# The last attention's gates as 24 more columns of its query, key and value product

## The reference

```python
h = x * rsqrt(mean(x * x, -1) + 1e-06) * norm_w
q, k, v = heads(Wq), heads(Wk), heads(Wv)          # h @ W.T, 128 columns each, 8 heads of 16
q, k = _apply_rope(q, cos, sin), _apply_rope(k, cos, sin)
beta, ig, og = gate(Wbeta, bbeta), gate(Wig, big), gate(Wog, bog)   # sigmoid(h @ W.T + b), 8 columns each
# over the tokens of a sequence:
M = M * f_t + g_t * scale * (k_t[:, None] * v_t[None, :])
y_t = (q_t @ M) * o_t
y = y @ Wout.T + bout
```

## Time and profile before

| what | before |
|---|---|
| median of 3 runs | 1366.78 us (1364.93 to 1370.55) |
| profiled execution | 1362.23 us, span of its instructions 1360.4 us |
| busy, share of the span | TensorE 88%, VectorE 78%, ScalarE 59%, GpSimd 50% |
| mean granted TensorE clock | 0.957 |

### The profile page before, as it was taken

How to read it: one execution, slowest core, us unless ns; L and a number is a source line. 1 busy time by engine, 2 the same in 40 slices (tenths; PEclk the granted TensorE clock), 3 DMA queues, 4 the chain that set the end, 5 groups by cost and what they waited for, 6 DMA issues and landing times.

```text
span 1360.4 us, 39548 instructions
## 1 busy us (share of the span) xinstructions
PE 1202.4 (88%) x14377; PEld 906.5 (67%) x14377; DVE 1059.4 (78%) x3479; ACT 808.9 (59%) x1351; POOL 678.0 (50%) x727
## 2 busy tenths in 40 slices
PE   2857888899889888888987899999989999999997
PEld 1524766676767666666766677877777777677765
DVE  4888789988787988798878787775786688876662
ACT  1545667546745655545655686675866566656562
POOL 0167657777677776778777653314243255210010
PEclk9987998999999998999998999999989899899897
DMA  9002433432344232223434321221200010000001
GB/s 317 1 32 65 112 99 86 121 93 89 97 124 124 64 100 69 83 75 86 105 93 116 89 62 37 57 56 46 55 25 26 10 41 25 25 11 9 11 2 32
DMA packets 172958, 94.13 MB, mean 69 GB/s; under 512 B 98539, under 2 KB 163206, under 8 KB 172646
## 3 DMA queue, kind: packets, MB, share of 16 engines
q1 hardware_dynamic: 112838, 34.26, 10.4%
q0 software_dynamic: 16384, 33.59, 8.8%
q10 hardware_dynamic: 43552, 23.74, 5.9%
HBM read 25.98 MB, written 45.61 MB: 53 GB/s over the span
## 4 chain that ended last, share of the span: by engine, by line
PE 46%; DVE 28%; ACT 9%; issue 6%; POOL 5%; SPq 3%; DMA 2%; ACTq 0%; POOLq 0%; DVEq 0%
PE bank L701 12%; PE bank L746 4%; PE bank L760 3%; POOL rows L1714 3%; SPq L1780 2%; DVE heads_store L975 2%; DVE x L1007 2%; PE sums L934 2%; PE bank L717 2%; PE bank L556 2%; PE bank L917 2%; PE bank L729 1%; DVE stats_head L964 1%; PE bank L748 1%; PE bank L786 1%
## 5 line engine op out<-in xcount | busy, mean ns | idle before, releaser
L1731 POOL DMA_INDIRECT y_in<-ys,r_result x256 | 276.8, 1081 | 131.4 <-issue 71.2
L1714 POOL DMA_INDIRECT rows<-store,r_slot x256 | 261.9, 1023 | 84.7 <-issue 76.1
L701 PE MATMUL bank<-u_xp,w_hi 128*128 128x128 f16 x2432 | 271.1, 225 | 15.3 <-DMA u_xp<-rows 4.4
L701 PE MATMUL bank<-u_xp,w_lo 128*128 128x128 f16 x1216 | 247.3, 222 | 0.0
L701 PEld LDWEIGHTS bank<-u_xp,w_hi 128*128 x2432 | 166.4, 99 | 64.0 <-issue 24.4
L701 PEld LDWEIGHTS bank<-u_xp,w_lo 128*128 x1216 | 119.8, 99 | 3.0
L1683 POOL TENSOR_SCALAR ve_front<-mv_front 128x4 f32<-128x4 f32 x16 | 3.1, 194 | 180.6 <-DVE mv_front L968 180.4
L556 PE MATMUL bank<-heads_store,w_hi 128*128 128x512 f16 x256 | 81.1, 400 | 7.2 <-DVE x L1043 3.1
L1484 ACT COPY heads_store<-bank 128x512 f32<-128x512 f32 x64 | 37.2, 586 | 73.8 <-PE bank L506 52.8
L746 PE MATMUL bank<-heads_store,f_w1s 128*128 128x512 f32 x128 | 74.7, 667 | 0.9 <-ACT heads_store L1591 0.9
L1007 DVE SCALAR_TENSOR_TENSOR x<-y_in,r_weight,x 128x128 f32<-128x128 f32 x256 | 72.6, 345 | 1.7 <-DMA y_in<-ys,r_result 0.5
(11 more groups left out here) (389 smaller groups left out, 3257.4 us busy)
## 6 DMA issues: line engine op xcount, KB each, us to landing
ys<-u_y_even ACTq DMA_DIRECT2D x38, 256.0 KB
ys<-u_y_odd ACTq DMA_DIRECT2D x38, 256.0 KB
u_xp<-rows SPq DMA_TRANSPOSE x304
x<-x_dram SPq DMA_DIRECT2D x16, 256.0 KB, 5.6
rows<-store,r_slot POOLq DMA_INDIRECT x256
y_in<-ys,r_result POOLq DMA_INDIRECT x256
out_dram<-x SPq DMA_DIRECT2D x16, 256.0 KB, 2.3
rows<-blank SPq DMA_DIRECT2D x48, 64.0 KB
```

Of the source, the lines that this page charges most:

```text
L701: ins = pe.matmul(B[:, of_block[j]], of_expert(wp, e, 2 * part + which), xp_rows[:, xp, of_block[j]], start=(n == 0 and j == 0), stop=(n = ...
L1714: pool.indirect_dma_start(row_dram[g], bass.IndirectOffsetOnAxis(route.slot[g][:, i, t:t + 1].bitcast(U32), 0), rows[:, groups[g].first * ...
L1731: pool.indirect_dma_start(fetch.y[i][:, t, k, :], None, y_dram[g], bass.IndirectOffsetOnAxis(route.result[g][:, k, t0 + t:t0 + t + 1].bitc ...
```

## The change

The two weights become one tile of 408 columns, and TensorE makes for each of the four tiles of tokens one product of 408 columns in place of one of 24 and one of 384; the gates are columns 384 to 407 of each of the four banks. VectorE reads them there with four instructions that multiply by `rstd` and add the bias at once, in place of one multiplication and one addition over all four tiles. ScalarE's copies of a bank also ask for VectorE's instruction on that bank, but a later one of it has been waited for by then. The written order of the steps (`turns`) stays.

```diff
-        a1_wqkv = sb("a1_wqkv", [P, 3 * D])
-        a1_wg = sb("a1_wg", [P, 3 * NH1])
-        a1_mean = sb("a1_mean", [P, 3 * D + 3 * NH1])
+        a1_w = sb("a1_w", [P, 3 * D + 3 * NH1])
+        a1_wqkv, a1_wg = a1_w[:, 0:3 * D], a1_w[:, 3 * D:]
...
-                    pe.matmul(M[:, 64:64 + 3 * D], minus_mean[:], a1_wqkv[:], start=True, stop=True)
-                    prep.by_tensor.mark(pe.matmul(M[:, 64 + 3 * D:64 + 3 * D + 3 * NH1], minus_mean[:], a1_wg[:],
-                                                  start=True, stop=True), "a1")
+                    prep.by_tensor.mark(pe.matmul(M[:, 64:64 + 3 * D + 3 * NH1], minus_mean[:], a1_w[:], start=True,
+                                                  stop=True), "a1")
...
                 elif k == 1:
-                    G = 3 * NH1
                     on.wait_ge(*s.by_scalar.at("xt", "attn1", c))
-                    B = bank(s.name, "z", c)
                     on.wait_ge(*prep.by_vector.at("a1_centred"))
                     for t in range(T):
-                        ins = pe.matmul(B[:, t * G:(t + 1) * G], s.xt[:, by_t[t]], a1_wg[:], start=True,
-                                        stop=True)
-                    s.by_tensor.mark(ins, "z", c)
-                    ring.free_at((s.name, "z", c), s.by_vector, "z", c)
-                    for t in range(T):
                         B = bank(s.name, "qkv", c, t)
-                        s.by_tensor.mark(pe.matmul(B[:, 0:3 * D], s.xt[:, by_t[t]], a1_wqkv[:], start=True,
+                        s.by_tensor.mark(pe.matmul(B[:, 0:3 * D + 3 * NH1], s.xt[:, by_t[t]], a1_w[:], start=True,
                                                    stop=True), "qkv", c, t)
                         ring.free_at((s.name, "qkv", c, t), s.by_scalar, "v", c, t)
...
-                    dve.tensor_tensor(a1_wg[:], a1_wg[:], mean[:, 3 * D:], ALU.add)
-                    mark(dve.tensor_tensor(a1_wqkv[:], a1_wqkv[:], mean[:, 0:3 * D], ALU.add), "a1_centred")
+                    mark(dve.tensor_tensor(a1_w[:], a1_w[:], mean, ALU.add), "a1_centred")
...
                 elif k == 1:
-                    on.wait_ge(*s.by_tensor.at("z", c))
                     on.wait_ge(*s.by_pool.at("rstd", "attn1", c))
-                    mark(dve.tensor_tensor(s.z, ring[s.name, "z", c][:, 0:T * G].rearrange(
-                        "p (t g) -> p t g", t=T), wide(s.rstd[:], G), ALU.mult), "z", c)
-                    on.wait_ge(*at("z", c))
-                    mark(dve.tensor_tensor(s.z, s.z, const["a1_bg"][:].unsqueeze(1).broadcast_to([P, T, G]),
-                                           ALU.add), "zb", c)
-                    on.wait_ge(*at("zb", c))
+                    for t in range(T):
+                        on.wait_ge(*s.by_tensor.at("qkv", c, t))
+                        mark(dve.scalar_tensor_tensor(s.z[:, t, :], ring[s.name, "qkv", c, t][:, 3 * D:3 * D + G],
+                                                      s.rstd[:, t:t + 1], const["a1_bg"][:], ALU.mult, ALU.add),
+                             "z", c, t)
+                    on.wait_ge(*at("z", c, T - 1))
                     mark(dve.tensor_scalar(s.zc, s.z, Z_LEAST, None, ALU.max), "zc", c)
...
                         on.wait_ge(*s.by_tensor.at("qkv", c, t))
+                        on.wait_ge(*s.by_vector.at("z", c, t))
                         scale = s.rstd[:, t:t + 1]
```

More of the change, by code:

```diff
@@ L1078, in prepared @@
                 elif k == E + 3:
-                    dve.tensor_scalar(a1_wqkv[:], const["a1_wqkv"][:], const["a1_nw"][:], None, ALU.mult)
-                    mark(dve.tensor_scalar(a1_wg[:], const["a1_wg"][:], const["a1_nw"][:], None, ALU.mult), "a1")
+                    dve.tensor_scalar(a1_wqkv, const["a1_wqkv"][:], const["a1_nw"][:], None, ALU.mult)
+                    mark(dve.tensor_scalar(a1_wg, const["a1_wg"][:], const["a1_nw"][:], None, ALU.mult), "a1")
                     dve.tensor_tensor(f1_w1s[:].rearrange("p (e h) -> p e h", e=E),
```

## The result

The changed kernel took **1392.3 us** (median of four runs, 1390.11 to 1403.94) against 1367.2 (four runs, 1364.93 to 1370.55) for the kernel before: a ratio of 1.0199, 95% interval 1.0138 to 1.0259. I had said 1371, with a range up to 1379. Repeated later beside fifteen runs of the kernel before, it had 1.0207 (1.0154 to 1.0259). So it is slower by 25 us where I forecast 4, and outside the range. The profiled execution took 1393.23 us, its span is 1391.4 (1360.4 before).

The account below looks back on a forecast made before the run. TensorE was taken to set the pace, though the chain also leaves it for VectorE. Chunk shifts of +6.9, -1.9 and -0.9 us, with TensorE's saving counted, gave +4.1 on the median 1366.78: 1371, range 1359 to 1379 (8 in 10).

Parts of the forecast that it names:

- TensorE's saving: TensorE, last attention: small gates' group gone, wider products added, 0.87 us less a chunk, 13.9 us in 16.
- The small instructions: VectorE, gates: four 24-column instructions cost 0.4 to 0.68 us against 0.59, no difference worth a term.
- The delay of the clamp: VectorE, gates: the clamp waits for the last wide product and ends 1.54 us later in chunk 12.
- VectorE's wait at these instructions: Sign: VectorE's waits at the four small instructions, ended by the wide product, sum to near 8.1 us plus about 15.
- The room: Room m between the end of the gated keys and TensorE's first transpose, 0.06 to 1.16 us in eight chunks.
- d: Each chunk's clamp delay, less VectorE's independent idle time before the gated keys; TensorE's shift is d - m, at best -0.87.
- The clock: Rival, TensorE: more waiting may bring one more 10 us stretch at half speed, +5 us, 1376; 15%.
- The sum: Last attention, 16 chunks: TensorE's shifts of 6.9 - 1.9 - 0.9 give +4.1 us.
- TensorE alone decides: Rival, last attention: TensorE, 97% busy, keeps half or all of the 13.9 us saving, 1353 to 1360; 15%.
- the full length of the wait: Rival, fourth bank: other instructions behind the clamp have consumers with less room; without room 13.6 us, 1374 to 1380; 20%.
- the keys' transposes waited: Sign, TensorE: the transposes of the gated keys wait for VectorE in eight chunks.
- TensorE's sum: Sign: TensorE's sum from 766 us on falls by some 14 us.

Follow-up runs that it names:

- e2: Changed kernel, but VectorE reads the gates of all four tiles from the first bank and waits for the first wide product alone; 1367.8 us, ratio 0.9999.
- e3: Kernel before, with four small VectorE instructions reading the small group's bank in place of one multiplication and one addition; 1370.5 us, ratio 1.0021.
- the filled kernel: Changed kernel with 38 unread multiplies of 512 columns added on TensorE ahead of six waits for normalized tokens; 1389.6 us, ratio 1.0173.
- e7: Changed kernel, but with the small products as before in chunks 0, 2, 6 and 10; ratio 1.0133 on the chip that takes 1.25 times as long.

## Why the prediction was wrong, step by step

- **TensorE's saving**, forecast 0.87 us a chunk: measured in chunk 12, from the first product's start to the end of the wide group, 3.01 us against 0.92 + 2.83 = 3.75, so 0.74. The column price was right (0.18 us for the added columns, 0.16 forecast); the small group, taken at 1.03, was 0.92 up to the start of the wide one. Small, but e2 shows the larger error: the saving came through in chunk 7 and almost nowhere else. I had credited it in every chunk with room.
- **The small instructions**: 242 ns each in the median, not 0.17 to 0.18. Only the last counts, 0.06 us. The Trainium skill's formula, "VectorE: DVE Perf Modes", section on the TRN2 errata, which gave my estimate of 150 ns, is too low here by 90; e3 shows that it costs nothing.
- **The delay of the clamp**, forecast 1.54 us in the bound chunks: measured 1.63 (3.53 against 1.91). Right. VectorE's wait at these instructions, forecast 8.1 + 15 = 23.1 us, is 21.6, 39 times:

```profile
DVE heads_store L1367 <- PE bank L777: 21.6, 39, 2.5
```

- **The room**: this is the step that failed. I took for each chunk the room m between the gated keys and their transposes, as if nothing in between needed what was delayed, and let TensorE use it and its saving. The shift of the keys' transposes against the first product, in us (chunks with no lower clock in that stretch in either trace):

| chunk | 0 | 2 | 3 | 4 | 5 | 7 | 8 | 10 | 12 | 13 | 15 | sum |
|---|---|---|---|---|---|---|---|---|---|---|---|---|
| forecast | 0 | -0.2 | 0 | -0.7 | -0.9 | -0.2 | +0.7 | +0.5 | +1.4 | -0.9 | +1.1 | +0.8 |
| measured | +0.07 | +0.30 | +0.96 | +0.23 | +1.33 | -0.02 | +1.62 | +0.60 | +1.56 | -0.64 | +1.62 | +7.6 |

  Chunks 10, 12 and 13, where I had no room or a great deal, are right to 0.3. In chunks 5 and 8, where I had counted on room and saving, 3.1 us are missing: TensorE stops earlier there, at a step of another chunk (for the gelu at L1584 in chunk 5, for the decays' multiplication at L1448 in chunk 8), for a bank or an input behind the same wait. The two rows of TensorE's timeline:

```profile
998.56 0.38 PE L754 MATMUL bank<-by_expert,heads_store 128*128 128x128 bf16 x4 [1.20 <-ACT heads_store L1584]
...
1102.54 0.66 PE L505 MATMUL bank<-w_packed,heads_store 128*128 128x128 f32 x4 [1.18 <-DVE store L1448]
```

  In chunks 3 and 4 another 1.9 us: there I had put d at 0 to 0.3, and the clamp came 1.6 us later (1.9 to 3.5 behind the first product), so I had misread which wait ended last. The rival that named just this ("other instructions behind the clamp have their own consumers on TensorE, some with less room") had 20%; its mechanism is the one that holds, its 1374 to 1380 are not.
- **The clock**: chunk 9 prices it. The stretch from the first product to the keys' transposes took 16.50 us before, 17.10 in the filled kernel (no lower clock in it), 21.38 in the repeated trace (10.2 us at the lower level) and 26.18 in the first (20.4 us). So (21.38 - 17.10) / 10.2 = 0.42 and (26.18 - 17.10) / 20.4 = 0.45 us for each us at the lower clock. Other places give less or a little more: 0.33 in chunk 12 and 0.37 in chunk 15 between the two traces of the changed kernel, 0.49 in chunk 7 between the two of the kernel before, and 0.35 over the whole part by the changed kernel's two ((628.0 - 618.3) / (105.8 - 78.5)). Row of the first trace behind the wait of 1.37 us at L885 (last line of the waits above):

```profile
1130.00:1150.00 20.00, 20.00 (x206) 14.10 (x205) 12.63 (x39) 6.96 (x11) 10.81 (x10) 0.50 0.11 28
```

  From the first product on there are 78.5 - 44.4 = 34.1 us more of it, at 0.35 to 0.45 some 12 to 15 us. My sum had put this term at nothing, and my rival at 5: it is the second step that failed.
- **The sum** between the two traces: the length from the first product to the end grew by 618.35 - 593.79 = 24.6 us. 12 to 15 is the clock, which leaves 10 to 13 for the waits themselves, against +4.1 forecast and the 13.6 that I had for the delays with no room at all. The other 6.4 us of the spans' 31.0 come before the first product (766.65 and 773.09 us), where the change does nothing and the lower clock took 13.6 us more (85.3 against 71.7); in the repeated trace of the kernel before, that part had 95.6 and the products began at 770.1. It is scatter of the clock, and the medians differ by 25, not 31.
- **TensorE alone decides**, 15%, 1353 to 1360: fallen, by e2 (1367.8), where the gates' wait was as short as before.
- **The chances**: I treated the full length of the wait and the clock as alternatives, 1374 to 1380 or 1376. They come together, since the one makes the gaps that go with the other. With the waits at 10 to 13 us and the clock at 15 to 12, 1366.8 + 25 = 1392; this divides what was measured, and doesn't forecast it. A range that let both happen at once had to reach there.

Of what I had named as signs: the waiting in front of VectorE's small instructions was right, TensorE's idle time rose by 20.4 us (18 forecast) and the wide group was 2.86 and 2.95 us on the chain in chunks 11 and 12 (2.83 forecast); the keys' transposes waited three times, not eight; TensorE's sum didn't fall by 14, since the lower clock added more than the change took off.

## What to carry to other kernels

A busy share of 97% doesn't make an engine the limit: ask which chain, across the other engines, ends each stretch of it, and take work off that chain or nothing is won. When a step is made to wait for later data, don't measure its room at its own last consumer only; go through everything that is queued behind it on its engine and on its readers' engines, take the least room among them, and count none of it twice. And where TensorE's clock moves during a dense kernel, price the waits twice, once for themselves and once for the time at the lower clock that goes with them; here the second was about as large as the first.

## What the runs showed of the hardware

- Each microsecond at the lower granted clock cost 0.42 to 0.45 us in chunk 9, 0.33 to 0.49 in three other places and 0.35 over the whole part: less than the half that TensorE loses, where it has to wait for VectorE or ScalarE anyway.
- A few waits of TensorE of 1.4 to 2.3 us in a stretch that is otherwise full were followed by 10 to 20 us at the lower clock in which it never idled. The same wait was followed by 20.4 us in one trace and 10.2 in the other, and one of 2.33 us by none within 10 us. In the filled kernel the wait at the place of the 1.37 us was 1.20, and no such stretch followed.
- Stretches at the lower clock also began with no idle time in the ten microseconds before (at 1072.03 us in the trace before; 3.4 to 6.8 us long in the traces here), so filling the waits doesn't remove all of it; why those begin stays open.
- One chip of those used takes 1.25 times as long for every kernel. On it the clock is at the lower level for 512 to 581 us of some 1700 (116 and 164 in the first two traces here), and the first 766 us, with the gathering and scattering of rows, are stretched to over 1010. The table by stage from 100 to 400 us, first e7 there, then the changed kernel on its own chip:

```profile
100.00:400.00 300.00, 207.20 (x1837) 151.80 (x1838) 198.71 (x671) 136.66 (x205) 153.31 (x163) 0.80 0.27 71
```

```profile
100.00:400.00 300.00, 254.43 (x2577) 190.86 (x2576) 253.02 (x840) 182.60 (x277) 205.08 (x214) 0.95 0.38 96
```

  TensorE gets 1837 records done there in place of 2577 and every engine is less busy, so more than the clock is slower; what, the runs don't tell.
